# A two-layer convolution kernel on one core: per-image products placed behind a whole half convolution, upper matrix halves cast by ScalarE, 58 side columns, the second filter loaded and split during the load phase

## What is computed

```python
    def _L0_conv_ref(x, w_in, b_in, kg_w1, kg_b1, kg_w2, kg_b2, w_out, b_out):
        xh = _conv1x1(x, w_in, b_in)
        pooled = jnp.mean(xh, axis=(2, 3))
        hcx = jax.nn.relu(pooled @ kg_w1.T + kg_b1)
        kernels = (hcx @ kg_w2.T + kg_b2).reshape(b, c, K, K)
        y = jax.lax.conv_general_dilated(x_r, k_r, window_strides=(1, 1), padding=((1, 1), (1, 1)), feature_group_count=b * c, ...)
        y = y * jnp.tanh(jax.nn.softplus(y))
        return _conv1x1(y, w_out, b_out)
    ...
    x = x + _L0_conv_ref(_gn(x), ...)
    x = x + _L1_conv_ref(_gn(x), ...)
```

## Time and profile before

| | us |
|---|---|
| median of 3 runs (3797.97 to 3801.11) | 3799.29 |
| the profiled execution | 3798.16 |
| its span, first to last instruction | 3796.4 |
| PE busy | 3658.1 (96%) |
| DVE busy | 3522.8 (93%) |
| ACT busy | 3316.2 (87%) |
| POOL busy | 2774.9 (73%) |

### The profile page before, as it was taken

The page is one execution under the profiler, slowest core; times in us unless marked ns, Lnnn a source line. Parts: engine busy times, 40 slices in busy tenths (PEclk is TensorE's granted clock), DMA queues, the critical chain, the costliest instruction groups (busy, mean ns, idle before and its releaser), DMA issues. The chain is left out here.

```text
span 3796.4 us, 65618 instructions
## 1 busy us (share of the span) xinstructions
PE 3658.1 (96%) x21868; PEld 2251.8 (59%) x21868; DVE 3522.8 (93%) x4778; ACT 3316.2 (87%) x5860; POOL 2774.9 (73%) x2388
## 2 busy tenths in 40 slices
PE   4899999999999999999999999999999999999997
PEld 2455666656566666666656666565666656666664
DVE  5999999999999999999999999999999999999996
ACT  3888989899898998989999898998989989897775
POOL 3566777877778777777777777777777777777773
PEclk8999999999999999999999999999999999999999
DMA  4323444444444444444444444444444444443333
GB/s 152 78 70 104 130 128 132 125 130 131 122 139 119 137 127 127 136 122 132 126 128 132 128 130 125 131 133 123 134 128 129 130 125 134 125 131 95 92 94 126
DMA packets 148159, 468.99 MB, mean 124 GB/s; under 512 B 17328, under 2 KB 18416, under 8 KB 147568
## 3 DMA queue, kind: packets, MB, share of 16 engines
q1 hardware_dynamic: 110960, 397.66, 30.1%
q0 software_dynamic: 36864, 67.13, 12.2%
HBM read 397.61 MB, written 134.22 MB: 140 GB/s over the span
## 5 line engine op out<-in xcount | busy, mean ns | idle before, releaser
L654 PE MATMUL psA<-hi,wa 128*128 128x288 f16 (+4 forms) x9792 | 1852.2, 280 | 0.8 <-DVE wtmp L876 0.8
L907 DVE SCALAR_TENSOR_TENSOR accB<-xh,vectors,accB 128x1024 f32<-128x1024 f32 x1280 | 1640.4, 1282 | 0.0
L1118 POOL TENSOR_TENSOR tsum<-tsum,tprod 128x1024 f32<-128x1024 f32 x512 | 1210.5, 2364 | 293.9 <-ACT tprod L407 271.2
L919 DVE SCALAR_TENSOR_TENSOR accS<-side,vectors,accS 128x448 f32<-128x448 f32 x2048 | 1399.1, 683 | 19.2 <-ACT accS L416 10.0
L654 PE MATMUL psA<-lo,wa 128*128 128x288 f16 (+5 forms) x4896 | 1320.6, 279 | 0.0
L654 PEld LDWEIGHTS psA<-hi,wa 128*128 128x128 f16 x9792 | 931.0, 98 | 336.6 <-issue 66.9
L696 PE MATMUL psBO<-wm,woutt 128*128 128x512 f32 x2048 | 966.4, 594 | 12.5 <-DVE X L929 11.8
L1122 POOL TENSOR_TENSOR X<-X,zt 128x512 f32<-128x512 f32 x480 | 610.9, 1273 | 363.3 <-DVE accB L907 289.5
L696 PEld LDWEIGHTS psBO<-wm,woutt 128*128 128x128 f32 x2048 | 385.4, 190 | 497.5 <-issue 496.6
L1110 POOL TENSOR_TENSOR lo<-X,hi 128x1024 f16<-128x1024 f32 x256 | 546.9, 2136 | 182.6 <-DMA hi<-in_x_dram 111.4
L407 ACT ACTIVATE tprod<-xh,vectors 128x1024 f32<-128x1024 f32 x512 | 583.2, 1139 | 32.6 <-POOL tsum L1118 32.5
(11 more groups left out here) (166 smaller groups left out, 3363.4 us busy)
## 6 DMA issues: line engine op xcount, KB each, us to landing
X<-in_x_dram SPq DMA_DIRECT2D x256, 512.0 KB, 3.3
out_dram<-X SPq DMA_DIRECT2D x256, 512.0 KB, 2.6
XS<-in_x_dram SPq DMA_DIRECT2D x240, 512.0 KB, 3.3
hi<-in_x_dram POOLq DMA_DIRECT2D x256, 256.0 KB, 4.3
X<-in_w_t_dram SPq DMA_DIRECT2D x2, 1152.0 KB, 18.3
w1t<-in_w_t_dram SPq DMA_DIRECT2D x1, 256.0 KB, 2.7
wint<-in_w_in_t_dram SPq DMA_DIRECT2D x1, 128.0 KB, 2.3
woutt<-in_w_out_t_dram SPq DMA_DIRECT2D x1, 128.0 KB, 2.6
```

Of the source, the lines that this page charges most:

```text
L654: last = mm(o[:, r:r + q, 0:cols], w, src[:, at:at + q, SIDE + dx - 1:SIDE + dx - 1 + cols], start=(tap == ORDER[0] and w is wh and src is ...
L907: V.scalar_tensor_tensor(out=rows_of(accB[:]), in0=xh[:, 8 * j + dy:8 * j + dy + 8, dx:dx + W], scalar=kk[i % 2][:, TAPS + k:TAPS + k + 1] ...
L919: V.scalar_tensor_tensor(out=side_out(), in0=side[:, 8 * j + dy:8 * j + dy + 8, dx:dx + SIDE], scalar=kk[i % 2][:, k:k + 1], in1=side_out( ...
L1118: P.tensor_tensor(tsum[:], tsum[:], tprod[:], ALU.add).then_inc(s_ta, 1)
```

## The change

SIDE goes from 56 to 58, so CW goes from 72 to 70: the convolution matmuls read 280 (or 276) columns in place of 288 (or 284), the side products 472 in place of 456, and the side taps 464 elements in place of 448. `small_0` moves behind all nine taps of `conv(n,0)`. The upper halves of the tap matrices and of the product matrices are cast by ScalarE (`taps_high`, `weights_high`) and no longer by GpSimd, whose `taps_low` and `weights_low` keep the subtraction. On ScalarE `tap_product(n+1,1)` comes ahead of the small copies, and `kernels_out` behind `mish_conv(n,0)`. w2 is loaded behind the constants, ahead of strips 2 to 15; ScalarE casts it ahead of the first chain, and VectorE subtracts its two halves ahead of `bn_stats` 16 and 20. Three GpSimd products by a per-partition scalar become products with a broadcast operand.

```diff
-SIDE = 56
+SIDE = 58
@@ sync
-            for k in range(2):
-                eng.dma_start(w2t[:, k], w2_t[:, k]).then_inc(s_w2in[k], 16)
+                    for k in range(2):
+                        eng.dma_start(w2t[:, k], w2_t[:, k]).then_inc(s_w2in[k], 16)
@@ scalar
+            def taps_high(i, u):
+                eng.wait_ge(s_wt, 3 * i + u + 1)
+                act(wa[:, i % 2, 0, 3 * u * C:3 * (u + 1) * C], wtmp[:], ACT.Copy).then_inc(s_wsh, 1)
+
+            def weights_high(i):
+                eng.wait_ge(s_wn, i + 1)
+                act(wb[:, i % 2, 0, :], wn[:], ACT.Copy).then_inc(s_wbh, 1)
...
-            stats_group("x", 0, small_bank(0))
-            pooled_out(0, small_bank(0))
-            hidden_out(0, small_bank(0))
             for k in range(2):
                 eng.wait_ge(s_w2in[k], 16)
                 act(w2p[:, 0, k], w2t[:, k], ACT.Copy).then_inc(s_w2h, 1)
+            stats_group("x", 0, small_bank(0))
+            pooled_out(0, small_bank(0))
+            weights_high(0)
+            hidden_out(0, small_bank(0))
             kernels_out(0, small_bank(0))
             bias_out(0, small_bank(0))
+            for u in range(3):
+                taps_high(0, u)
...
                     tap_product(n + 1, 0)
+                if s == 0 and b >= 1:
+                    taps_high(b, 2)
+                if n + 1 < N:
+                    tap_product(n + 1, 1)
                 if s == 12 and build:
+                    weights_high(b + 1)
                     pooled_out(b + 1, small_bank(1))
                 if s == 3 and b >= 1:
                     layer1_bias(b - 1, small_bank(1))
-                if n + 1 < N:
-                    tap_product(n + 1, 1)
+                if s in (14, 15) and build:
+                    taps_high(b + 1, s - 14)
+                mish_conv(n, 0)
                 if s == 13 and build:
                     kernels_out(b + 1, small_bank(1))
-                mish_conv(n, 0)
@@ tensor
-                conv(n, 0, slice(0, 5))
+                first = n % STRIPS == 0
+                conv(n, 0, slice(0, 6 if first else TAPS))
                 small_0(n)
-                first = n % STRIPS == 0
-                conv(n, 0, slice(5, 6 if first else TAPS))
@@ vector
             for c in range(2 * STRIPS):
+                if c in (16, 20):
+                    k = (c - 16) // 4
+                    eng.wait_ge(s_w2h, k + 1)
+                    V.tensor_tensor(w2p[:, 1, k], w2t[:, k], w2p[:, 0, k], ALU.subtract).then_inc(s_w2l, 1)
@@ gpsimd
-                P.tensor_scalar(wn[:], wint[:], st["x"]["r"][:, 0:1], None, ALU.mult).then_inc(s_wn, 1)
+                P.tensor_tensor(wn[:], wint[:], st["x"]["r"].broadcast_to([C, HID]), ALU.mult).then_inc(s_wn, 1)
...
-            def taps_halves(i, u):
-                k, part = 3 * i + u + 1, slice(3 * u * C, 3 * (u + 1) * C)
-                eng.wait_ge(s_wt, k)
-                P.tensor_copy(wa[:, i % 2, 0, part], wtmp[:]).then_inc(s_wsh, 1)
-                eng.wait_ge(s_wsh, k)
+            def taps_low(i, u):
+                part = slice(3 * u * C, 3 * (u + 1) * C)
+                eng.wait_ge(s_wsh, 3 * i + u + 1)
                 P.tensor_tensor(wa[:, i % 2, 1, part], wtmp[:], wa[:, i % 2, 0, part], ALU.subtract).then_inc(s_wsl, 1)
...
                 if s == 0 and b >= 1:
-                    taps_halves(b, 2)
+                    taps_low(b, 2)
                 if m >= 1:
                     add(m - 1, 1)
                 if n + 2 < N:
```

More of the change, by code:

```diff
@@ L946, in _ @@
             V.tensor_scalar(valid[:], valid[:], -1.0, None, ALU.add).then_inc(s_valid, 1)
-            for k in range(2):
-                eng.wait_ge(s_w2h, k + 1)
-                V.tensor_tensor(w2p[:, 1, k], w2t[:, k], w2p[:, 0, k], ALU.subtract).then_inc(s_w2l, 1)
             for u in range(3):
@@ L1067, in kernel_bias @@
                 eng.wait_ge(s_pl, i + 1)
-                P.tensor_scalar(bk[:], k2[:, 0:TAPS], bp[i % 2][:, 0:1], None, ALU.mult).then_inc(s_bst, 1)
+                P.tensor_tensor(bk[:], k2[:, 0:TAPS], bp[i % 2][:, 0:1].broadcast_to([C, TAPS]), ALU.mult).then_inc(s_bst, 1)
                 eng.wait_ge(s_bst, 2 * i + 1)
@@ L1073, in kernel_bias, with weights_low @@
                 P.tensor_tensor(bx[:, 32:32 + TAPS], bk[:], bh[:], ALU.subtract).then_inc(s_bxr, 1)
-            def taps_halves(i, u):
-                k, part = 3 * i + u + 1, slice(3 * u * C, 3 * (u + 1) * C)
-                eng.wait_ge(s_wt, k)
-                P.tensor_copy(wa[:, i % 2, 0, part], wtmp[:]).then_inc(s_wsh, 1)
-                eng.wait_ge(s_wsh, k)
+            def taps_low(i, u):
+                part = slice(3 * u * C, 3 * (u + 1) * C)
+                eng.wait_ge(s_wsh, 3 * i + u + 1)
                 P.tensor_tensor(wa[:, i % 2, 1, part], wtmp[:], wa[:, i % 2, 0, part], ALU.subtract).then_inc(s_wsl, 1)
-            def weights_halves(i):
-                eng.wait_ge(s_wn, i + 1)
-                P.tensor_copy(wb[:, i % 2, 0, :], wn[:]).then_inc(s_wbh, 1)
+            def weights_low(i):
                 eng.wait_ge(s_wbh, i + 1)
@@ L1088, in fold_1 @@
             def fold_1(i):
-                P.tensor_scalar(lpt[:, i % 2, :], lt[:], st["1"]["r"][:, 0:1], None, ALU.mult).then_inc(s_lpt, 1)
+                P.tensor_tensor(lpt[:, i % 2, :], lt[:], st["1"]["r"].broadcast_to([C, C]), ALU.mult).then_inc(s_lpt, 1)
             def high(n):
@@ L1134, in _ @@
             pool_bias(0)
-            weights_halves(0)
+            weights_low(0)
             hidden_low(0)
@@ L1138, in _ @@
             for u in range(3):
-                taps_halves(0, u)
+                taps_low(0, u)
             for k in range(1, EXTRA + 1):
@@ L1163, in slot @@
                 if s in (14, 15) and build:
-                    taps_halves(b + 1, s - 14)
+                    taps_low(b + 1, s - 14)
                 if m >= 0:
@@ L1177, in slot @@
                 if s == 12 and build:
-                    weights_halves(b + 1)
+                    weights_low(b + 1)
                 if s == 1 and b >= 1:
```

## The result

The changed kernel takes 3812.13 us (median of 7 runs, 3809.83 to 3816.39); the kernel before, run beside it, 3800.75 (7 runs, 3797.97 to 3801.81). The ratio is 1.0034, with a 95% interval of 1.0022 to 1.0045: slower by 11.4 us. The span of the profiled execution is 3810.3 us, before 3796.4. The time lies inside the range of the prediction, but the forecast was 3801 and "within 0.2%"; what came is "slower by over 0.2%".

A forecast was written before the change was run, and what follows sets the result against it. PE (TensorE) was taken to bound ordinary slots, VectorE close behind. From 3798.16, -31.0 + 2.0 + 1.3 - 2.7 - 3.5 + 23.7 + 11.7 = +1.5 gives 3799.7, as a median 3801; 8-in-10 range 3776 to 3817.

The forecast's parts named there:

- PE bounds the ordinary slot, VectorE has 0.07 us behind it: Ordinary slots: PE falls from 13.72 to 13.56 us and stays the bound; VectorE's lap rises to 13.49.
- Rival E: Convolution matmuls: columns are not what a matmul costs, so ordinary slots gain nothing; 3830 us, chance 0.06.
- 58 columns, -27.7: Side columns: 0.16 us less in 194 ordinary slots, -31.0, with +2.0 for slots 2 and 11 and +1.3 for VectorE-bound slots.
- Slots 3 and 12, -0.18 and -0.25: Chain slots: PE's gaps close but the wait moves to the cast; only GpSimd's shorter folds gain, -2.7 and -3.5 us.
- Rival B: Slots 3 and 12: the gaps close for good, giving 1.4 and 0.9 us, another 27 us; 3774, chance 0.07.
- Slot 0, +23.7: Slot 0: ScalarE's late upper-half copy makes the first product_b wait 2.2 us; 1.7 us more in 14 images.
- rival A: Slot 0 does not grow, as ScalarE copies earlier or the 2.2 us are swallowed; 3777 us, chance 0.15.
- Slots 14 and 15, 0: The same copies in slots 14 and 15: VectorE's idle time takes the delay; 0, at most 1 us an image.
- rival D: VectorE becomes the bound; slot 14's late spread reaches PE through the residual, 15 times 1 us; 3816, chance 0.22.
- Load phase, +11.7: Start: kernels(0) 6.9 us later from early w2, then 4.9 from ScalarE's upper copies ahead of its evacuations; bounds +5 and +15.
- rival C: Load phase costs only the reordered copies, since w2 fills lost DMA time; 3789 us, chance 0.13.
- The split into 5.6 and 4.3: Load phase: w2's load delays strips by 5.6 us, VectorE's two subtractions add 4.3; statistics end 9.9 us later.

The follow-up runs named there:

- a_slot0_pool: Changed kernel, but in slot 0 of an image GpSimd again casts the last third's upper half: 3781.45 us, ratio to the kernel before 0.9944.
- c_best: Kernel before with 58 side columns, products behind the half convolution and two folds with a broadcast operand; w2 and upper halves as before: 3769.5 us, ratio 0.9914.
- b_side58: Kernel before with SIDE = 58 as the only edit: 3779.06 us, ratio 0.9937.

## Why the prediction was right, and where it was short

- **PE bounds the ordinary slot, VectorE has 0.07 us behind it.** Right: 13.56 us; VectorE's lap in image 0 is 13.50 (13.49 predicted). Rival E (no gain from columns) is out.
- **58 columns, -27.7.** Mis-sized: 23.6 by the run with this edit alone. Two things are missing. One is in the count of 13 ordinary slots an image, some 2 us over images 2 to 14: slot 1 gains nothing in either kernel, and in the changed one slot 14 gives 0.05 and slot 13 nothing. PE waits 0.17 us in slot 1 and 0.11 in slot 13 ahead of `product_side`, and there fewer columns seem only to lengthen the wait. Slots 2 and 11, booked at half, gave all. The other is the scattered long slots, 4.7 us in the trace of that run (0.9 in that of the changed kernel), of which the prediction has nothing.
- **Slots 3 and 12, -0.18 and -0.25.** Right, -0.21 and -0.33; folds and move together gave 9.6 us between two runs, where 6.2 were booked. The wait moved to `product_b` and `product_side` as the chain in the prediction had it, and the gain is GpSimd's shorter fold. Rival B is out.
- **Slot 0, +23.7.** The mechanism was right and the wait of 2.2 us near it (`product_b` 2.4 later, 2.06 idle), rival A is out; the size was short, and this is the step that missed by most. The slot grew by 1.94 and not 1.69, 27 us in 14 images, and the clock behind the wait, a term that the prediction didn't have, took another 5. Priced by the two runs it is 31 to 34 us.
- **Slots 14 and 15, 0.** Right: VectorE idles 0.80 us at its second tap matrices, 0.86 before, and slot 14 got no longer. The time is nearer to rival D's 3816 than to the forecast, but not by D's mechanism.
- **Load phase, +11.7.** 12.7 at the first tap; rival C is out. The split into 5.6 and 4.3 for the statistics was close (11.0, of which the subtractions are 4.2 by the run that moved them), the load of w2 a little dearer. The prediction carried the first tap's delay to the end in full. `a_slot0_pool` against `c_best` bears this out with 13.0 us at the end for 13.9 at the first tap; the two runs that took 4 and 8 us of it away changed the median by less, 0 and 3.7, and can't decide it.

The 11.4 us can be put together from runs, each taken against the kernel before beside it: the columns -23.6 (`b_side58`; -27.7 was booked), folds and move -9.6 (`c_best` less that; -6.2), load phase and the other upper copies +13.0 (`a_slot0_pool` less `c_best`; +11.7), slot 0 +31.6 (the changed kernel less `a_slot0_pool`; +23.7). The terms miss by +4.1, -3.4, +1.3 and +7.9 us. So one miss hid part of the others. Each of these differences is uncertain by some 5 to 7 us by the intervals, and of the misses only that of slot 0 is larger; there the slot's length and the clock's rows show it too.

By slots, against the forecast of 3801: 0.43 us an image in slots 0, 1, 13 to 15 less what 2, 3, 11 and 12 gave more, 5.6 in thirteen images; five low stretches, 5; the load phase, 1.0; the rest is within an us.

## What to carry over

A small cast moved to an engine that is "less busy" has to be priced by where it stands in that engine's queue, and by everything queued behind its consumer: here 0.5 us of ScalarE work cost 31 us. A wait of an engine that doesn't bound its slot may still be owed in the next long slot: look for waits of the chain's engine one or two slots ahead of the gap, and move the load that they are for. Before an instruction is moved off the front of a queue, ask what lands while it runs.

## What the runs showed of the chip

- TensorE idle for 2.06 us in slot 0, in the rows above, was followed by half clock (0.51) for some 3.4 us in 4 to 6 of some 14 places, at 1.0 us each.
- GpSimd stood while VectorE worked: 5.08 us for a step of 0.20, beside two subtractions of 5.01 together.
- A load issued by GpSimd took 5.2 us from its issue to the cast that waited for it in `c_best` (1241.11 to 1246.32), and 7.15 where three loads were issued within 0.9 us of one another.
